# Three of eight key chunks of the attention product as fp16 halves

## The reference, cut to what matters

```python
x = x + _L0_attn_ref(_layernorm(x), Wq, Wkv, Wout, ...)
x = x + _L0_ffn_ref(_layernorm(x), ...)        # 16 experts, gated attention
# in _L0_attn_ref: 16 score maps of 1024 x 1024 in each of 4 batches
dots = jnp.einsum('bhqd,bhkd->bhqk', q, k)      # D = 32
attn_w = jax.nn.softmax(dots, axis=-1)
attn_w = attn_w[:, :, 0] - lam * attn_w[:, :, 1]
attn = jnp.einsum('bhqk,bhkd->bhqd', attn_w, v) # 64 columns of v
rms = jnp.sqrt(jnp.mean(attn * attn, axis=-1, keepdims=True))
attn = gamma * (attn / (rms + EPS)) * (1.0 - LAMBDA_INIT)
```

## Time and profile before

| | us |
|---|---|
| median of 3 runs | 1581.05 (1579.9 to 1581.23) |
| the profiled execution, its own time | 1579.55 |
| its span, from first to last instruction | 1577.7 |

### The profile page before, as it was taken

One profiled execution on the slowest core, in us unless ns is written; L12 is line 12 of the kernel. 1 busy time (PEld: TensorE's weight loads), 2 busy tenths in 40 slices (PEclk: granted clock), 3 DMA queues, 4 the chain that ended last, 5 costly groups with the idle time before them and its releaser, 6 DMA issues. The chain is left out here.

```text
span 1577.7 us, 57787 instructions
## 1 busy us (share of the span) xinstructions
PE 1461.3 (93%) x25906; PEld 1170.8 (74%) x25906; DVE 996.4 (63%) x1375; ACT 851.8 (54%) x1693; POOL 500.6 (32%) x432
## 2 busy tenths in 40 slices
PE   2599999999999999999999999999962899999997
PEld 1267777777777777777777777777752799989997
DVE  5576676766767666676766667676327466656665
ACT  2056556566655565655555656555633455545553
POOL 4202333233342323334232333422233433323330
PEclk9789999999999999999999999999985999999999
DMA  3201011010101011010110101010001000000000
GB/s 99 50 16 43 11 35 23 23 34 12 43 13 33 23 24 39 6 43 13 33 29 17 43 6 39 19 27 3 3 18 38 3 9 7 8 7 8 8 9 9
DMA packets 37042, 36.54 MB, mean 23 GB/s; under 512 B 14273, under 2 KB 24257, under 8 KB 36801
## 3 DMA queue, kind: packets, MB, share of 16 engines
q1 hardware_dynamic: 36288, 32.62, 8.7%
q10 hardware_dynamic: 512, 0.26, 0.1%
HBM read 5.33 MB, written 2.10 MB: 5 GB/s over the span
## 5 line engine op out<-in xcount | busy, mean ns | idle before, releaser
L1085 DVE TENSOR_REDUCE part_max<-ring_ps 128x2 f32<-128x1024 f32 x512 | 625.4, 1224 | 349.9 <-PE ring_ps L557 340.9
L506 PEld LDWEIGHTS att_ps<-v_sb,pT 128*64 128x64 f32 x16384 | 632.2, 138 | 145.4 <-issue 30.1
L506 PE MATMUL att_ps<-v_sb,pT 128*64 128x65 f32 x16384 | 650.9, 222 | 2.5 <-issue 2.5
L808 ACT ACTIVATE pT<-st_ps 128x512 f32<-128x512 f32 x1024 | 553.6, 609 | 159.6 <-PE st_ps L490 152.9
L490 PE MATMUL st_ps<-qa,ka 98*64 98x512 f16 x2048 | 397.2, 386 | 0.0
L557 PE MATMUL ring_ps<-ka,qa 96*64 96x512 f16 x2048 | 311.9, 385 | 27.9 <-DMA ka<-split 19.1
L460 POOL TENSOR_TENSOR xs<-xnT,rw_all 128x2048 f32 (+1 forms) x32 | 115.5, 3610 | 209.6 <-PE t_ps L659 202.8
L816 ACT ACTIVATE raw_attn<-att_ps 128x260 f32<-128x260 f32 x128 | 49.6, 387 | 205.6 <-PE att_ps L506 205.6
L490 PEld LDWEIGHTS st_ps<-qa,ka 98*64 98x64 f16 x2048 | 115.1, 109 | 60.9 <-issue 9.7
L673 PE MATMUL qkv_ps<-ew_split,xsT 128*128 128x192 f16 x1536 | 143.8, 248 | 4.3 <-DVE xsT L1253 4.3
L557 PEld LDWEIGHTS ring_ps<-ka,qa 96*64 96x64 f16 x2048 | 95.8, 112 | 65.0 <-issue 30.8
(11 more groups left out here) (193 smaller groups left out, 1338.1 us busy)
## 6 DMA issues: line engine op xcount, KB each, us to landing
qa<-split SPq DMA_DIRECT2D x192, 64.0 KB, 2.0
ka<-split SPq DMA_DIRECT2D x192, 64.0 KB, 2.0
resid<-in_L_attn_x SPq DMA_DIRECT2D x4, 512.0 KB, 7.4
out<-yo SPq DMA_DIRECT2D x32, 64.0 KB, 1.5
qa<-shift_rows ACTq DMA_DIRECT2D x64, 4.0 KB
wkv_sb<-in_L_attn_Wkv SPq DMA_DIRECT2D x1, 512.0 KB, 5.4
ew<-in_L_ffn_q_proj SPq DMA_DIRECT2D x1, 512.0 KB, 5.7
ew<-in_L_ffn_k_proj SPq DMA_DIRECT2D x1, 512.0 KB, 7.4
```

The lines of the kernel that those rows point to most:

```text
L506: mm = pe.matmul(att_ps[q0:q0 + TILE_COLS, qt * DV1:(qt + 1) * DV1], pT[:, blk % 2, kt, qt * P + q0:qt * P + q0 + TILE_COLS], v_sb[:, j % ...
L808: act.activation(pT[:, blk % 2, kt, :], st_ps[:, c % ST_BANKS, :], ACT.Exp).then_inc(exp_ok, 1)
L1085: dve.tensor_reduce(part_max[:, which % 2, 2 * quarter + m // 2, m % 2, :], pair.rearrange("p (n k) -> p n k", n=2), AX.X, ALU.max, negate ...
```

## The change

Chunks kt = 0, 1 and 2 of every block (`SPLIT_CHUNKS = 3`) reach the product with V as sums of fp16 halves instead of fp32. The weights of such a chunk are `p_half` (high half and rest of the exponentials), the moving operand is `v_half` (the same of V). Each unit n of these chunks becomes three fp16 matmuls in each column tile: high times high (65 columns), high times rest (64), rest times high (65). The other five chunks stay fp32. The order of the chunks within a query tile becomes 3, 4, 5, 6, 7, 0, 1, 2.

Who makes the halves: ACT copies `pT` to the high half (`high_half`), one slot after the exponential and behind the next one; POOL subtracts it for the rest (`low_halves`), at the head of its work for a block. V's high half is a second ACT copy out of the same PSUM pair as `v_sb`, and POOL forms the rest once a step (`low_values`). So that halves don't fall below fp16's range, the exponentials are scaled by 1024: `shifts` adds ln 1024 to the shift with one more small DVE instruction a group, and the factor cancels in the division by the softmax sum.

```diff
+SPLIT_CHUNKS = 3
+KT_ORDER = tuple(range(SPLIT_CHUNKS, 8)) + tuple(range(SPLIT_CHUNKS))
+EXP_SCALE = 1024.0
 # POOL
+            pool.memset(v_half[:, :, 0, :, :, DV:DV1], 1.0).then_inc(parts_set, 1)
+            def low_halves(blk):
+                for kt in range(SPLIT_CHUNKS):
+                    pool.wait_ge(high_ok, SPLIT_CHUNKS * blk + kt + 1)
+                    pool.tensor_tensor(p_half[:, blk % 2, 1, kt, :], pT[:, blk % 2, kt, :], p_half[:, blk % 2, 0, kt, :],
+                                       ALU.subtract).then_inc(low_ok, 1)
+            def low_values(j):
+                pool.wait_ge(v_low_ok, 2 * j + 1)
+                pool.wait_ge(ring_A, EMPTIED["A"][RING_INDEX["v", j] + 1])
+                pool.tensor_tensor(v_half[:, j % 2, 1, :, :, 0:DV], v_sb[:, j % 2, :, :, 0:DV], v_half[:, j % 2, 0, :, :, 0:DV],
+                                   ALU.subtract).then_inc(v_low_ok, 1)
             for kb in range(FIRST_BLOCK, END_BLOCK):
+                if 0 <= kb < BLOCKS:
+                    low_halves(kb)
+                if (kb + 1) % 8 == 0 and 0 <= (kb + 1) // 8 < STEPS:
+                    low_values((kb + 1) // 8)
 # PE, in values
-                    qt, kt = divmod(n, 8)
+                    qt, kt = n // 8, KT_ORDER[n % 8]
+                    if n == 8 - SPLIT_CHUNKS:
+                        pe.wait_ge(v_low_ok, 2 * (j + 1))
+                        pe.wait_ge(low_ok, SPLIT_CHUNKS * (blk + 1))
+                        for k, (p_part, v_part) in enumerate(SPLIT_PRODUCTS):
+                            cols = DV if v_part else DV1
+                            for q0 in range(0, P, TILE_COLS):
+                                mm = pe.matmul(att_ps[q0:q0 + TILE_COLS, qt * DV1:qt * DV1 + cols],
+                                               p_half[:, blk % 2, p_part, kt, qt * P + q0:qt * P + q0 + TILE_COLS],
+                                               v_half[:, j % 2, v_part, kt, r // 2, 0:cols], start=False,
+                                               stop=closes and k == 2)
 # ACT
+            def high_half(c):
+                blk, kt = divmod(c, 8)
+                if kt < SPLIT_CHUNKS:
+                    act.wait_ge(exp_ok, c + 1)
+                    act.activation(p_half[:, blk % 2, 0, kt, :], pT[:, blk % 2, kt, :], ACT.Copy).then_inc(high_ok, 1)
                     act.activation(v_sb[:, which % 2, :, :, 0:DV], pair.rearrange("p (t h d) -> p t h d", t=NT, h=2),
+                                   ACT.Copy).then_inc(v_low_ok, 1)
+                    act.activation(v_half[:, which % 2, 0, :, :, 0:DV], pair.rearrange("p (t h d) -> p t h d", t=NT, h=2),
                                    ACT.Copy).then_inc(ring_A, 1)
                         exponentials(8 * kb + s)
+                        if s:
+                            high_half(8 * kb + s - 1)
 # DVE, in shifts
+                dve.tensor_scalar(shift32[:, buf, :, :], shift32[:, buf, :, :], math.log(EXP_SCALE), None,
+                                  ALU.add).then_inc(shift_ok, 1)
```

More of the change, by code:

```diff
@@ L157, in block_kernel @@
         pT = sb("pT", [P, 2, NT, HALF])
+        p_half = sb("p_half", [P, 2, 2, SPLIT_CHUNKS, HALF], F16)
+        v_half = sb("v_half", [P, 2, 2, NT, 2, DV1], F16)
         part_max = sb("part_max", [P, 2, 8, 2, 2])
@@ L228, in block_kernel @@
         recip_ok, tail_P = sem("recip_ok"), sem("tail_P")
+        high_ok, low_ok, v_low_ok = sem("high_ok"), sem("low_ok"), sem("v_low_ok")
         rms_const_ok = sem("rms_const_ok")
@@ L344, in _ @@
             pool.wait_ge(parts_set, 1)
+            pool.memset(v_half[:, :, 0, :, :, DV:DV1], 1.0).then_inc(parts_set, 1)
+            pool.wait_ge(parts_set, 2)
             units = ka[:, :, :, :].rearrange("p a r t -> p (a r t)").bitcast(F32)
             pool.memset(units[K_MAX:K_ALL, :], PAIR_OF_ONE).then_inc(parts_set, 1)
-            pool.wait_ge(parts_set, 2)
+            pool.wait_ge(parts_set, 3)
             pool.memset(units[K_MAX:K_MAX + 1, :], PAIR_OF_UNIT).then_inc(parts_set, 1)
-            pool.wait_ge(parts_set, 3)
+            pool.wait_ge(parts_set, 4)
             def tokens(ap):
@@ L504, in values @@
                         pe.wait_ge(ring_A, EMPTIED["A"][RING_INDEX["v", j] + 1])
[L505 to L508, removed]
+                    if n == 8 - SPLIT_CHUNKS:
+                        pe.wait_ge(v_low_ok, 2 * (j + 1))
+                        pe.wait_ge(low_ok, SPLIT_CHUNKS * (blk + 1))
+                    opens, closes = n % 8 == 0, n % 8 == 7
+                    if kt >= SPLIT_CHUNKS:
+                        for q0 in range(0, P, TILE_COLS):
+                            mm = pe.matmul(att_ps[q0:q0 + TILE_COLS, qt * DV1:(qt + 1) * DV1],
+                                           pT[:, blk % 2, kt, qt * P + q0:qt * P + q0 + TILE_COLS],
+                                           v_sb[:, j % 2, kt, r // 2, :], start=opens, stop=closes)
+                    else:
+                        for k, (p_part, v_part) in enumerate(SPLIT_PRODUCTS):
+                            cols = DV if v_part else DV1
+                            for q0 in range(0, P, TILE_COLS):
+                                mm = pe.matmul(att_ps[q0:q0 + TILE_COLS, qt * DV1:qt * DV1 + cols],
+                                               p_half[:, blk % 2, p_part, kt, qt * P + q0:qt * P + q0 + TILE_COLS],
+                                               v_half[:, j % 2, v_part, kt, r // 2, 0:cols], start=False,
+                                               stop=closes and k == 2)
                 if last == 32:
@@ L560, in ring @@
                 elif kind == "shift":
-                    pe.wait_ge(shift_ok, 3 * (which + 1))
+                    pe.wait_ge(shift_ok, 4 * (which + 1))
                     if which == 0:
@@ L586, in _ @@
                         if c == 0:
-                            pe.wait_ge(parts_set, 3)
+                            pe.wait_ge(parts_set, 4)
                         chunk(c)
@@ L1106, in shifts @@
                                   AX.X, ALU.min).then_inc(shift_ok, 1)
-                dve.wait_ge(shift_ok, 3 * g + 1)
+                dve.wait_ge(shift_ok, 4 * g + 1)
+                dve.tensor_scalar(shift32[:, buf, :, :], shift32[:, buf, :, :], math.log(EXP_SCALE), None,
+                                  ALU.add).then_inc(shift_ok, 1)
+                dve.wait_ge(shift_ok, 4 * g + 2)
                 whole = shift32[:, buf, :, :].rearrange("p (t h) s -> p t (h s)", h=2)
                 dve.tensor_scalar(shift16[:, buf, :, 0, :], whole, 1.0 / SHIFT_UNIT, None, ALU.mult).then_inc(shift_ok, 1)
-                dve.wait_ge(shift_ok, 3 * g + 2)
+                dve.wait_ge(shift_ok, 4 * g + 3)
                 dve.scalar_tensor_tensor(out=shift16[:, buf, :, 1, :], in0=shift16[:, buf, :, 0, :], scalar=-SHIFT_UNIT,
```

## The result

| | before | after |
|---|---|---|
| median, us | 1580.5 (1579.9 to 1581.2) | 1616.7 (1616.5 to 1619.0) |
| span of the profiled execution | 1577.7 | 1614.9 |
| ratio | 1 | 1.0235, 95% interval 1.0222 to 1.0247 |

What follows compares the result with a forecast made beforehand. PE was taken to bound the attention, with everybody waiting for it. Against 1579.55 us, -41.5 + 1.0 + 2.9 + 2.3 + 13.8 + 1.5 = -20.0 gave 1559.55, or 1561 us for the median; range 1545 to 1655.

Steps and rivals of the forecast that it cites:

- shifts gains one instruction of about 0.18 us a group on DVE: DVE's shift: the added instruction costs nothing, as DVE idles a third of the time and works over three slots ahead.
- POOL's rests: POOL, head of each block: 483 us more on 342 busy, yet consumers still served with 1 us or more to spare.
- Rival 1: PE's product: the small-matmul floor adds up over column tiles, 51.6 ns a pair, 1653 us; chance in full 22 in 100.
- The 4 ns: PE's product: matmuls of different column tiles start some 4 ns apart, which would leave 30 ns a pair.
- Rival 2: ACT in the way more than counted, delaying later exponentials: 15 to 35 us more, 1576 to 1596; chance 16 in 100.
- PE's term: PE's product with V: each converted unit takes 90 ns, 27 less than now; 1536 units save 41.5 us.
- blocks 3, 4 and 5: PE, slot 1: two saved units precede a chunk that waits for ACT anyway; 0.054 us lost each time, 2.3 us.
- ACT's high halves: ACT, three copies a block of 615 ns: PE waits 0.06 us in block 7, 0.21 in block 3; 1.0 and 2.9 us.
- V's second copy: ACT, copy out of the ring before exponential 1: 0.92 us unhidden in 15 blocks, 13.8 us, the largest single cost.
- The three steps with early norms: Early norms add 3.8 us on POOL, three times, so PE's `cols` comes some 0.5 us late: 1.5 us.

Runs made afterwards that it cites:

- `before_pool_load`: Kernel before, plus three 128x512 POOL subtractions at the head of each block whose results nobody reads: 1585.1 us, ratio 1.0025.
- `pe_only`: Changed kernel with constants for all halves, so without ACT's high halves, V's high half and POOL's rests: 1566.7 us, ratio 0.9914.
- turned order: Changed kernel, ln 1024 added as shift rows leave PSUM, V's high half copied in slot 7, every second query tile's chunks ordered 0 to 7: 1571.8 us.
- `v_later`: Changed kernel with V's high half copied on ACT from `v_sb` in slot 7 instead of out of the ring: 1604.8 us, ratio 1.0148.
- `combine_first`: Changed kernel with POOL's `combine` ahead of the rests, and POOL waiting in blocks 2 and 6 until the shift is made: 1597.5 us, ratio 1.0111.
- `before_load_op`: Kernel before, plus three POOL subtractions a block and a third small DVE instruction in each group's shift: 1603.9 us, ratio 1.0148.

## Why the prediction was wrong

**The step that failed: "shifts gains one instruction of about 0.18 us a group on DVE", at no cost, and POOL's rests weighed only by who waits for them.** I checked POOL's lateness against each consumer and found 1 us of room; that held (but for the three steps below, PE hardly waits for POOL). I did not ask what a busy POOL does to DVE while it runs. In the changed kernel `tensor_scalar`, `tensor_tensor` and `scalar_tensor_tensor` instructions of 0.17 us with all operands in SBUF, started behind the start of a POOL instruction on large tiles, last until it ends, up to 1.09 us; the large reductions out of PSUM do not change (1223 ns against 1224). The trace of before had a row of it, which I passed over: a DVE instruction on 128x8 elements, in the steps with early norms, beside POOL's products of 1.9 us:

```profile
L1005 DVE TENSOR_TENSOR gs<-gs x5: 169/1905/1910, 434.7 to 1191.3; 128x8 f32<-128x8 f32 x4, 128x32 f32<-128x32 f32 x1
```

The Trainium skill has a rule for this in "Advanced Engine Details and Errata" (Mode Summary): VectorE's second SBUF port is shared with GpSimd, and GpSimd instructions and VectorE instructions in its two-port modes block each other. The trace agrees for `tensor_scalar`. That `tensor_tensor` and `scalar_tensor_tensor` are held as well, that section does not say; the rows show it. `tensor_reduce` is not held. A place where one POOL instruction meets a reduction and a `tensor_scalar`, all within SBUF:

```profile
436.57 2.15 POOL L448 TENSOR_TENSOR v_half<-v_sb,v_half 128x1024 f16<-128x1024 f32 x1
436.90 1.21 DVE L1187 TENSOR_REDUCE gs<-x2sq 128x8 f32<-128x1024 f32 x1
438.15 0.60 DVE L1188 TENSOR_SCALAR gs<-gs 128x8 f32<-128x8 f32 x1
```

The reduction ends 0.6 us ahead of POOL's instruction, after the 1.21 us that it always takes; the `tensor_scalar` ends with POOL's, at 438.75 against 438.72. Nor does every POOL instruction hold: beside POOL's power on 128x8 elements (L410, 1.65 us) a `tensor_scalar` took 0.17 us, three times of three.

With two instructions (`before_pool_load`) one hold was free. With three, the last fell into the next POOL instruction: 25 blocks at 1.03 and one at 0.61, **26.5 us**.

**Rival by rival.** Rival 1, the floor that adds up over tiles, would have given more than this (1653) and is refuted: pairs of fp16 matmuls go at 32 ns, 16 ns a matmul. So the 25 ns of the Trainium skill's "TensorE: Matmul & The Clock Gate" (Wait — 56ns, not 53.3ns?) do not hold across column tiles here. The 4 ns that the prediction took from the same page (The mechanism) are drawn there for row tiles; the changed kernel's trace agrees for column tiles too: the two of a pair start up to 5 ns apart, most often 3. Rival 2, ACT more in the way, has a small part at most: ACT cost 5.2 us in blocks 3 and 7, where 3.9 were forecast, and 3.6 in the last blocks, not 15 to 35 more. Neither rival names DVE beside POOL. The range of 1545 to 1655 held the time by luck: it reached that far for rival 1, which has no part in it.

**PE's term was mis-sized: 41.5 forecast, less 2.3 for blocks 3, 4 and 5, so 39.2; 20.7 measured** (the attention of `pe_only`). PE in block 47 of the changed kernel:

```profile
501.58 0.36 PE L544 MATMUL att_ps<-v_half,p_half 128*64 128x65 f16 x12
501.77 0.38 PE L516 MATMUL st_ps<-qa,ka 98*64 98x512 f16 x2
501.99 0.26 PE L544 MATMUL att_ps<-v_half,p_half 128*64 128x65 f16 x6
502.08 0.55 PE L537 MATMUL att_ps<-v_sb,pT 128*64 128x65 f32 x12
502.45 0.60 PE L596 MATMUL ring_ps<-ka,qa 96*64 96x512 f16 x4
```

Two converted units take 0.19, 95 ns each where I had 90. And three fp32 units right behind a converted one take 0.37, where three of 117 take 0.35: the way back costs. From `pe_only`: 12 units save 12 x 22 = 264 ns, the block is shorter by about 190, so each of the three switches within a slot costs 25. The turned order leaves one of three and gains two such prices, 50, a block; measured 40 to 100. In blocks 3, 4 and 5 the units saved in slot 1 are lost to a wait for ACT, as forecast, though 0.08 and not 0.054 each. The forecast counted units and forgot their neighbours. What in PE makes the switch cost something, no run here shows.

**ACT's high halves: right in mechanism and place.** A copy takes 647 ns (615 forecast), in the changed kernel. Block 3 waits 0.25 (9.18 against 8.94 in `pe_only`; forecast 0.21), block 7 0.09 (forecast 0.06). Missed were the last six blocks of the attention, which have no maxima left on PE: there ACT paces the block, and they take 3.6 us more than in `pe_only`.

**V's second copy: right.** Forecast 13.8; block 5 is 0.92 shorter in `v_later`, and its attention 14.0 us.

**The three steps with early norms**: forecast 1.5 in all, measured 7.2. Their blocks 0 and 1 (blocks 40 and 41 for the first) take 9.31 and 9.86 us, in `pe_only` 7.89 and 8.89. The 1.42 of block 40 are PE's `cols`, late for POOL as forecast, but by more than the 0.5 I had:

```profile
438.67 1.20 POOL L420 TENSOR_TENSOR attn_n<-attn,tl 128x256 f32<-128x256 f32 x2
440.01 0.63 PE L609 MATMUL ring_ps<-ident,attn_n 128*128 128x128 f32 x4 [1.10 <-DVE part_max L1134]
```

POOL's result is there at 439.87 and `cols` starts. The row names DVE's maxima, but the pair that `cols` writes was emptied at 436.99. The 0.97 of block 41 are DVE's short chain on the norms, which is held as well:

```profile
446.51 1.05 DVE L1052 TENSOR_TENSOR gs<-gs 128x8 f32<-128x8 f32 x1
447.60 1.09 DVE L1053 TENSOR_SCALAR gs<-gs 128x8 f32<-128x8 f32 x1
448.72 1.08 DVE L1054 TENSOR_TENSOR gs<-gs 128x8 f32<-128x8 f32 x1
```

Two experiments part them. In `combine_first` the chain meets POOL once, as in the kernel before (1.91 us): block 41 takes 8.89, block 40 still 9.29. In `before_pool_load` the chain is held three times and `cols` is in time: block 41 takes 1.01 more, block 40 only 0.09. So 4.3 us are POOL's `cols`, and 2.9 are held instructions once more.

The account of the attention, from the first to the last `raw_copy`: `pe_only` is 20.7 us shorter than before. Against `pe_only` the changed kernel has 26.5 (held shifts), 7.2 (early norms), 14.0 (V's copy), 3.8 and 1.4 (ACT's copies in blocks 3 and 7) and 3.6 (last blocks). That makes +35.8, which is what the two traces differ by (1100.8 against 1065.0 us); the start is 1.4 us later.

## What to carry to other kernels

When work is added to POOL, look not only for who waits for its results but for which short `tensor_scalar`, `tensor_tensor` and `scalar_tensor_tensor` instructions run beside it on DVE within SBUF: each may last until the POOL instruction in progress ends, and a chain of them meets one after the other. A change of two harmless parts can cost through their meeting, so try them alone and together. And price a converted matmul by a stream that contains its neighbours: the way from fp16 back to fp32 cost some 25 ns each time, as much as one unit saves (22).

## What the runs showed of the hardware that I had not expected

- A `tensor_scalar` of 128x16 within SBUF on DVE took 0.17 us with POOL idle and up to 1.06 with POOL in a subtraction or product on 128x512; `scalar_tensor_tensor` up to 1.18 (`before_load_op`). `tensor_reduce` and `reciprocal` within SBUF were not held (1.21 us and 0.19 us beside POOL), and POOL's power on 128x8 held nothing.
- Column-tile pairs of fp16 matmuls with 64 weights and 65 columns go at 32 ns a pair, though 24 untiled ones of 16 columns took 25.8 ns each: whatever sets the 25.8 does not add up over two column tiles.
- A per-partition bias on ACT's exponential of 128x512 costs 88 ns (705 against 617). The Trainium skill's "ScalarE: Activation LUTs" (What ACT_TABLE_LOAD costs) has about 93 ns for such an operand; the trace agrees within 5.
